# Encoder and cross attention in one program block, with batch 0's preparation queued inside the encoder's last step

## What is computed

```python
# 1. encoder of 6 layers: causal linear attention and an MLP, layer norm behind both
for l in range(N_LAYERS):
    q, k, v = x @ Wq[l] + bq[l], x @ Wk[l] + bk[l], x @ Wv[l] + bv[l]
    a = causal_linear_attn(elu(q) + 1, elu(k) + 1, v) @ Wo[l] + bo[l]
    x = layer_norm(x + a, g1[l], be1[l])
    x = layer_norm(x + gelu(x @ W1[l] + b1[l]) @ W2[l] + b2[l], g2[l], be2[l])
x = layer_norm(x, gf, bf)
x = _layernorm(x_in + x)
# 2. cross attention over ctx, 16 heads of 16, two softmax maps
attn = softmax(q1 k1 / scale) - gain * softmax(q2 k2 / scale)
o = attn @ vp                      # per head, then normalised per head
x = _layernorm(x + o @ wo.T)
# 3. feed-forward of three cycles
x = _layernorm(x + ffn(x))
```

## Time and profile before

| | us |
|---|---|
| median of 3 runs | 1772.83 (1771.63 to 1775.62) |
| the profiled execution | 1772.78 |
| its span | 1771.1 |
| TensorE busy | 1646.4 (93%) |
| VectorE busy | 1355.7 (77%) |
| ScalarE busy | 898.4 (51%) |
| GpSimd busy | 787.7 (44%) |
| DMA, mean over the span | 42 GB/s |

### The profile page before, as it was taken

How to read it: one execution, slowest core, us unless ns; L and a number is a source line. 1 busy time by engine, 2 the same in 40 slices (tenths; PEclk the granted TensorE clock), 3 DMA queues, 4 the chain that set the end, 5 groups by cost and what they waited for, 6 DMA issues and landing times. The chain is left out here.

```text
span 1771.1 us, 37461 instructions
## 1 busy us (share of the span) xinstructions
PE 1646.4 (93%) x15622; PEld 1330.7 (75%) x15622; DVE 1355.7 (77%) x2631; ACT 898.4 (51%) x1429; POOL 787.7 (44%) x580
## 2 busy tenths in 40 slices
PE   4899999999999999999999999999839999999598
PEld 4688888888888888888888888888725666665334
DVE  5778889888888888888888888888526777777346
ACT  2455554455554545545554455544216666665245
POOL 2343445434554435434553445533342555542325
PEclk8899999999999999999999999999959999999799
DMA  5100000100010000100001100100057777762001
GB/s 117 49 1 5 28 10 25 31 31 10 26 31 1 31 10 25 31 25 8 11 27 29 31 10 25 21 2 2 0 116 140 138 129 132 135 123 46 14 1 48
DMA packets 71704, 74.17 MB, mean 42 GB/s; under 512 B 18288, under 2 KB 57712, under 8 KB 71536
## 3 DMA queue, kind: packets, MB, share of 16 engines
q1 hardware_dynamic: 71536, 71.78, 19.6%
HBM read 57.08 MB, written 14.68 MB: 41 GB/s over the span
## 5 line engine op out<-in xcount | busy, mean ns | idle before, releaser
L629 POOL TENSOR_TENSOR e_h_lo<-e_h_f,e_h_hi 128x512 fp32r<-128x512 f32 x192 | 253.1, 1322 | 310.0 <-ACT e_h_hi L490 307.5
L714 DVE TENSOR_TENSOR e_am<-e_sc,c_amask 128x1024 f32<-128x1024 f32 x192 | 225.9, 1218 | 16.9 <-PE e_sc L365 16.6
L489 ACT ACTIVATE e_h_f<-e_pr,e_h_bias 128x512 f32<-128x512 f32 x192 | 132.2, 689 | 183.7 <-PE e_pr L166 179.6
L1394 DVE TENSOR_REDUCE x_mx<-x_psS 128x4 f32<-128x1024 f32 x128 | 155.0, 1221 | 66.3 <-PE x_psS L1112 65.9
L164 PE MATMUL e_pr<-e_yT_hi,e_W_hi 128*128 128x512 f32 x384 | 167.6, 437 | 0.3 <-DVE e_yT_lo L707 0.3
L164 PE MATMUL e_tr<-e_W_hi,e_h_hi 128*128 128x256 f32 x576 | 164.4, 285 | 1.4 <-issue 1.4
L166 PE MATMUL e_tr<-e_W_hi,e_h_lo 128*128 128x256 f32 x576 | 162.9, 283 | 0.0
L165 PE MATMUL e_tr<-e_W_lo,e_h_hi 128*128 128x256 f32 x576 | 161.6, 281 | 0.0
L1255 ACT ACTIVATE x_ex<-x_psT 128x1024 f32<-128x1024 f32 x128 | 131.1, 1024 | 57.8 <-PE x_psT L1138 56.9
L166 PE MATMUL e_pr<-e_yT_hi,e_W_lo 128*128 128x512 f32 x384 | 152.2, 396 | 0.0
L165 PE MATMUL e_pr<-e_yT_lo,e_W_hi 128*128 128x512 f32 x384 | 151.9, 396 | 0.0
(11 more groups left out here) (267 smaller groups left out, 4653.5 us busy)
## 6 DMA issues: line engine op xcount, KB each, us to landing
x_qs<-query_rows SPq DMA_DIRECT2D x128, 128.0 KB, 4.8
e_raw_m<-in_L_attn_W_dram SPq DMA_DIRECT2D x12, 1024.0 KB, 6.8
x_ks<-key_rows SPq DMA_DIRECT2D x64, 128.0 KB, 4.9
query_rows<-x_q_hi SPq DMA_DIRECT2D x16, 256.0 KB, 2.4
query_rows<-x_q_lo SPq DMA_DIRECT2D x16, 256.0 KB, 2.5
x_ctok<-in_ctx_dram SPq DMA_DIRECT2D x8, 256.0 KB, 5.4
x_xo<-in_x_dram SPq DMA_DIRECT2D x8, 256.0 KB, 2.8
key_rows<-x_k_hi SPq DMA_DIRECT2D x8, 256.0 KB, 4.9
```

Of the source, the lines that this page charges most:

```text
L489: act.activation(h_f[:, m % HR, :], ps_pr[m % 2][:, :], ACT.Gelu, bias=h_bias[:, m:m + 1])
L629: pool.tensor_tensor(h_lo[:, m, :], h_f[:, m % HR, :], h_hi[:, m, :].bitcast(F32), ALU.subtract).then_inc(h_lo_done, 1)
L714: dve.tensor_tensor(am[:, s % 2, c, :, :, :], ps_sc[:, :, c * 2 * P:(c + 1) * 2 * P].rearrange("p r (h n) -> p r h n", n=P), amask[:, :].u ...
L1394: dve.tensor_reduce(mx[:, N % 2, :, :].rearrange("p i (a h x) -> p h a i x", h=2, a=2)[:, pair, :, :, 0], ps_s[pair][:, :, :].rearrange("p ...
```

## The change

`cross` becomes `cross_stage`. It no longer opens a block; it returns functions for each engine, and the encoder's lists call them. So encoder and cross attention are one block without a meeting of the engines between them. The cross attention's tiles are now allocated from the right side of SBUF over the tiles that only the encoder's attention used (`att`), which nobody needs after step 22; SyncE waits for the last use of the two raw weight buffers before it loads `raw_wo`. The order of the PSUM tensors is changed so that `x_psS` lies on the four banks of `e_sc`: `early(0)` to `early(3)`.

- *Step 22:* VectorE makes the statistics of batch 0 ahead of the subtraction for `Wo`, and the block matrices (now one instruction) behind it.
- *Step 23, PE:* weights and context behind `mlp_down(1)`, values behind `mlp_down(3)`, transposes of x1 behind `mlp_up(1)`, the first query half behind `mlp_up(2)`, the second behind the step. The wait for the last gelu ahead of the last `mlp_down` is gone; `h_lo` is still waited for.
- *Step 23, the others:* as in the two places below. ScalarE copies weights, context and values ahead of the first gelu. The copies of x1 and of the queries for batch 0 go from ScalarE to VectorE. The zeroing of `vx` and `mx` goes from GpSimd to VectorE. The last `mlp_down`'s layer norm 2 is centred in slot 1 and scaled in slot 2. Batch 1's `encoder_norm` is split in `encoder_scale` and `encoder_add` and stands behind GpSimd's last `h_lo`.
- *Weights grouped:* the four weight products go to one bank and are copied at once, so are the two of the values and the four of `wo` (3 copies for 10).

```diff
+    att.close()
+    banks.close()
+    own.close()
+    nxt = cross_stage(nc, ctx, consts, X, inputs)
+    final = NT * L - 1
 
...
-            load_next(sp)
+            inputs.load(sp)
+            sp.wait_ge(o_lo, L)
+            sp.wait_ge(w2_lo, L)
+            nxt.sync(sp)
...
+                if u == final:
+                    pe.wait_ge(z_done[1], SB * NT * L)
+                    cross.weights()
+                    cross.context(0, cross.early(3))
...
+                if u == final:
+                    cross.values(0, cross.early(0))
...
                 if mlp:
                     mlp_up(0)
                     mlp_up(1)
+                if u == final:
+                    cross.x1_transpose(0, cross.early(1))
...
                     if mlp:
                         mlp_up(2 + s)
+                    if u == final and s == 0:
+                        cross.queries(0, 0, cross.early(2))
...
-            pe.wait_ge(yT_lo_done, 2 * NT * L)
-            pe.wait_ge(gelu_done, FC * NT * L)
+            cross.queries(0, 1, cross.early(3))
             for s in range(SB):
-                mlp_down(s, NT * L - 1, L)
+                mlp_down(s, final, L)
+            cross.items()
...
+                if u == final:
+                    cross.weights()
+                    cross.context(0, cross.early(3))
+                    cross.select()
...
+                    if u == final:
+                        cross.values(0, cross.early(0))
                     gelu(0)
...
+                if u == final:
+                    cross.encoder_scale(0)
                 if mlp:
                     rsqrt(1, ve_done[1], u + 1)
+                if u == final:
+                    pool.wait_ge(ln_done[1], SB * NT * L)
+                    cross.encoder_add(0)
+                    cross.x1_norm(0)
+                    cross.keys_lo(0)
...
+            cross.encoder_scale(1)
+            cross.encoder_add(1)
             rsqrt(2, ve_done[2], NT * L)
+            cross.items()
...
+                if u == final:
+                    residual(2, 0, d, last, m_full, xb2_done)
                 if mlp:
                     scale(1, u, q, rows_a["be1"])
+                if u == final:
+                    cross.sets()
...
-                if prev:
+                if prev and u < final:
                     residual(2, 0, d, last, m_full, xb2_done)
...
                 if prev:
                     residual(2, 1, d, last, m_full, xb2_done)
+                if u == final:
+                    cross.x1_stats(0)
+                    cross.value_weights()
+                if prev:
                     residual(2, 2, d, last, m_full, xb2_done)
...
+                if u == final:
+                    cross.x1_transposed(0, cross.early(1))
+                    cross.queries_hi(0, 0, cross.early(2))
+                    cross.queries_lo(0, 0, cross.early(2))
+                    scale(2, d, last, rows_m["be2"])
...
+                if u == final - 1:
+                    cross.encoder_stats(0)
...
+                if u == final - 1:
+                    cross.blocks()
...
+            cross.queries_hi(0, 1, cross.early(3))
+            cross.queries_lo(0, 1, cross.early(3))
+            cross.encoder_stats(1)
             for s in range(SB):
                 residual(2, s, final, NT - 1, m_full, xb2_done)
                 spread(2, s, final, NT - 1)
             moments(2, final)
-            centre(2, final, NT - 1, rows_m["g2"], ln2_rows_loaded, 32 * L)
-            scale(2, final, NT - 1, rows_m["be2"])
-
-    own.close()
+
+            def last_centre():
+                centre(2, final, NT - 1, rows_m["g2"], ln2_rows_loaded, 32 * L)
+
+            def last_scale():
+                scale(2, final, NT - 1, rows_m["be2"])
+
+            cross.items({1: last_centre, 2: last_scale})
+
+    nxt.own.close()
...
+    def early(i):
+        return ps_s[i // 2][:, i % 2, :]
...
+        def weights():
+            flat = bd[:, :, :, :].rearrange("p i h d -> p i (h d)")
+            pe.wait_ge(bd_done, 1)
             for k in range(MAPS):
                 for c in range(KC):
-                    pe.wait_ge(bd_done, (2 + k) * KC + c + 1)
-                    pe.matmul(bank(k * KC + c)[:, 0:P], bd[:, k * KC + c, :, :].rearrange("p h d -> p (h d)"),
-                              bd[:, (2 + k) * KC + c, :, :].rearrange("p h d -> p (h d)"), start=True, stop=True).then_inc(prep_full, 1)
+                    mm = pe.matmul(early(0)[:, blk(k * KC + c)], flat[:, k * KC + c, :], flat[:, (2 + k) * KC + c, :],
+                                   start=True, stop=True, skip_group_check=True)
+            mm.then_inc(prep_full, 1)
             for c in range(KC):
-                pe.wait_ge(bd_done, 4 * KC + c + 1)
-                pe.transpose(bank(4 + c)[:, 0:P], bd[:, 4 * KC + c, :, :].rearrange("p h d -> p (h d)"), ident[:, :]).then_inc(prep_full, 1)
+                mm = pe.transpose(early(1)[:, blk(c)], flat[:, 4 * KC + c, :], ident[:, :])
+            mm.then_inc(prep_full, 1)
             pe.wait_ge(wo_loaded, 16)
-            for n in range(KC):
-                for m in range(KC):
-                    i = n * KC + m
-                    if i >= 2:
-                        pe.wait_ge(prep_copied, i - 1)
-                    pe.transpose(bank(6 + i if i < 2 else i - 2)[:, 0:P], raw_wo[:, n, blk(m)], ident[:, :]).then_inc(prep_full, 1)
-            pe.wait_ge(prep_copied, 10)
-
-            def transpose_to(out, src):
-
+            for m in range(KC):
+                for n in range(KC):
+                    mm = pe.transpose(early(2)[:, blk(m * KC + n)], raw_wo[:, n, blk(m)], ident[:, :])
+            mm.then_inc(prep_full, 1)
...
+        def items():
             scores(0, 0)
+            pe.wait_ge(q_lo_done, KC)
             scores(0, 1)
...
+        def weights():
+            act.wait_ge(prep_full, 1)
+            act.activation(wqk[:, :, :, :].rearrange("p k c n -> p (k c n)"), early(0), ACT.Copy, scale=DH ** -0.5).then_inc(prep_copied, 1)
+            act.wait_ge(prep_full, 2)
+            act.activation(wv[:, :, :].rearrange("p c n -> p (c n)"), early(1)[:, 0:KC * P], ACT.Copy).then_inc(prep_copied, 1)
+            act.wait_ge(prep_full, 3)
+            act.activation(woT[:, :, :].rearrange("p c n -> p (c n)"), early(2), ACT.Copy).then_inc(prep_copied, 1)
...
+        def encoder_scale(e):
+            rsqrt(0, e)
+            pool.wait_ge(rows_loaded, 32)
+            if e > 0:
+                pool.wait_ge(x1_step, XS * (e - 1) + XS)
+            for s in range(QB):
+                pool.tensor_scalar(xw[:, s, :], X[:, e * QB + s, :], mv[0][:, s, 0:1], rs[0][:, s:s + 1],
+                                   ALU.subtract, ALU.mult).then_inc(x1_step, 1)
+            pool.wait_ge(x1_step, XS * e + QB)
+            pool.tensor_tensor(xw[:, :, :], xw[:, :, :], gf[:, :].unsqueeze(1).broadcast_to([P, QB, D]), ALU.mult).then_inc(x1_step, 1)
+
+        def encoder_add(e):
+            pool.wait_ge(xo_loaded, 16 * e + 16)
+            pool.tensor_tensor(xo[:, :, :], xo[:, :, :], bf[:, :].unsqueeze(1).broadcast_to([P, QB, D]), ALU.add).then_inc(x1_step, 1)
+            pool.wait_ge(x1_step, XS * e + QB + 2)
+            pool.tensor_tensor(xw[:, :, :], xw[:, :, :], xo[:, :, :], ALU.add).then_inc(xadd_done, 1)
...
+        def x1_transposed(e, bank):
+            dve.wait_ge(x1_tr, e + 1)
+            dve.tensor_copy(x1T[:, :, :].rearrange("p c n -> p (c n)"), bank).then_inc(x1T_done, 1)
+
+        def queries_hi(e, c, bank):
+            dve.wait_ge(q_full, KC * e + c + 1)
+            dve.tensor_copy(q_hi[:, c, :], bank).then_inc(q_hi_done, 1)
...
+        def blocks():
+            dve.wait_ge(w_loaded, 16 * 6)
+            dve.tensor_tensor(bd[:, :, :, :], raw_w[:, :, :, :].rearrange("p i c d -> p (i c) d").unsqueeze(2).broadcast_to([P, 5 * KC, HC, DH]),
+                              headmask[:, :].unsqueeze(1).unsqueeze(3).broadcast_to([P, 5 * KC, HC, DH]), ALU.mult).then_inc(bd_done, 1)
+            dve.tensor_scalar(neg_gain[:, :], gain[:, :], -1.0, None, ALU.mult)
...
+        def sets():
             dve.memset(first_rows[:, :, :], 0.0).then_inc(sets_done, 1)
-            encoder_stats(0)
+            dve.memset(vx[:, :, :, :, HX:HP], 0.0)
+            dve.memset(vx[:, :, :, :, DH:HX], 1.0)
+            dve.memset(mx[:, :, :, :], 0.0).then_inc(zeros_set, 1)
             dve.wait_ge(sets_done, 1)
             for pair in range(2):
                 for a in range(2):
                     r = a * HALF + pair * HP
                     m = dve.memset(first_rows[r:r + 1, pair, :], 1.0)
...
+        def value_weights():
+            w = wv[:, :, :].rearrange("p c (h d) -> p (c h) d", d=DH)
+            dve.wait_ge(prep_copied, 2)
+            dve.tensor_reduce(wv_sum[:, :], w, AX.X, ALU.add).then_inc(sets_done, 1)
+            dve.wait_ge(sets_done, 3)
```

(7 more changed lines are left out.)

728 lines of the change are left out of this document (338 added, 390 removed).

## The result

The changed kernel takes **1725.26 us** (median of 4 runs, 1723.98 to 1727.0), the kernel before 1773.92 in the same series (4 runs, 1771.63 to 1775.62): ratio 0.9727, 95% interval 0.971 to 0.9744. The profiled execution took 1723.98 us, its span 1722.3.

What follows compares the result with a forecast made beforehand. The bound was a 46.0 us engine-to-engine chain between the last encoder matmul and the first score matmul. Gain 46.0 - 6.9 (end of encoder) - 0.2 (after first score) = 38.9 us, from 1772.83 to 1733.9 us; range 1729 to 1742.

Steps and rivals of the forecast that it cites:

- the end of the encoder: Encoder's last two steps: taking in batch 0's preparation makes PE free for scores 6.9 us later.
- PE's moved work, 6.4: Encoder's last two steps: batch 0's products, transposes and query halves cost PE 5.8 us, 6.4 with changes of matmul kind.
- Step 22, +0.7, and `bd`: VectorE in step 22: batch 0's statistics delay PE 0.7 us; block matrices take about 1.5, 1.1 of it in idle time.
- The new wait, 1.6 instead of 0.6: Last step, before the MLP input's transposes: PE waits 1.6 us for VectorE's third residual instead of 0.6, +1.0.
- Given back, -1.4: Before the last `mlp_down`: the second query half fills PE's 1.40 us wait for the last gelu, -1.4.
- Queries in time, cover 0.8 to 2.8: At the first score: keys and query rows are back from DRAM 0.8 to 2.8 us before PE asks; nothing paid.
- After the first score, +0.2: First slots: residual and moments +0.9, centring and scaling 0 to 1, full PE clock -0.7; net +0.2 us.
- queries late: Rival, at the first scores: query chain slips by 8 us, idle PE falls to 1.2 GHz; 1740 us, chance 0.12.
- The stretched step: Rival, last encoder step: GpSimd blocks nine two-input VectorE operations, 1.04 us each, +9.4 us; 1743 us, chance 0.10.
- The slower clock through the whole cross attention: Rival: without its long rest PE stays at 1.2 GHz, 0.7 us per slot over 64 slots; 1777 us, chance 0.02.

Runs made afterwards that it cites:

- place_only: Kernel before with only the encoder's tiles put at the changed kernel's SBUF addresses: 1764.26 us, ratio 0.9943.
- zeros_later: Changed kernel with VectorE's zeroing of the cross attention's rows moved from ahead of the third residual to behind the first query half: 1722.40 us, ratio 0.971.

## Why the prediction was wrong

It failed on a sentence that had no number: "On both sides of it the kernel runs at its own pace, which the change does not touch." The encoder's 23 steps became 8.33 us faster in the profile, 9.4 us in the runs, by where its tiles stand. The diff showed the new allocation; the working read it only as memory for the cross attention. No rival had the encoder in it, so the range had no room: the forecast without it was 1733.9, and 1733.9 - 8.3 = 1725.6 against 1725.26 measured.

The rest came out at the forecast, by luck in part. From the row of step 22 to the end of the span the changed kernel takes 521.9 us and place_only, which has the same pace, 560.9: 39.0 us against 38.9. But the end of the encoder cost 5.8 us instead of 6.9, and behind the first score 1.6 us were lost (447.3 against place_only's 445.7) instead of 0.2; the two errors cancel. Term by term (times of the kernel after are compared with those before less the 8.33):

1. *PE's moved work, 6.4.* Too much: by start times it measured 1239.84 - 1237.94 = 1.90 for weights and context, 0.81 for the values, 0.36 for x1 and 0.67 and 0.68 for the two query halves, **4.4** in all. The query halves were priced at 2.0 and took 1.35, the transposes at 1.8 and took 1.37, the products at 2.0 and took 1.70. The changes of kind were there: the encoder's next matmul follows late behind each group (1255.66 - 1255.24 = 0.42 us behind the first query half, where 0.23 is usual), some 0.4 in all where 0.6 were expected.
2. *Step 22, +0.7, and `bd`.* Right for PE: it waited 1.75 us for the last query rotation, 0.76 more than the 0.99 of place_only. Too little for VectorE: the one instruction for `bd` took 2.48 us. The 1.5 did not follow from its rows, for the ten old ones took 2.31 together. So the first residual of the attention is 1.9 us late (1231.70 against 1238.09 - 8.33), where 0.7 and 0.4 were expected.
3. *The new wait, 1.6 instead of 0.6.* Right in kind, 2.43 us in size. The third residual is 4.2 us late, 4.8 were expected; PE was there sooner because its own work was shorter. The zeroing held the residual, as the step had it, but GpSimd's sum of the batch's input was ready only 0.4 us before VectorE was, as zeros_later shows.
4. *Given back, -1.4.* Right: no wait before the last `mlp_down`. The end of the encoder is 1275.15 - (1278.45 - 8.33) = 5.0 us late, not 6.9. This flatters the change a little, since the faster pace goes on behind the row of step 22; against place_only it is (1275.15 - 1200.39) - (1268.14 - 1199.16) = 5.8.
5. *Queries in time, cover 0.8 to 2.8.* In time, but only just. The eight loads were issued from 1264.30 on, the last one landed at 1274.44 by the trace, 0.6 us ahead of PE. SyncE's delay was there (7.2 us from store to loads), and PE came sooner than the working had it.
6. *After the first score, +0.2.* It was 1319.21 - 1275.04 = 44.2 us to the first scores of slot 9, against 1367.69 - 1324.45 = 43.2: **+0.9**. The moments did delay the first maxima by about 1 us. The full clock that should have given 0.7 was not there: after only 2.06 us of rest it fell to 0.50 for 10 us, and slot 1 took 1282.94 - 1277.85 = 5.09 us, exactly as before. It was back at 1.00 at 1288, behind 10 us of work with waits of under 0.5 us. The Trainium skill (TensorE: Matmul & The Clock Gate, "What's actually happening") says that activity releases the throttle; the trace agrees.

The rivals: queries late, not seen, though 0.6 us of cover is thin. The stretched step did not occur in the changed kernel (VectorE's four centring operations took 1.66 us), and occurred one small edit away; VectorE's scaling, four operations in 4.41 us, was slowed too but off the path. The slower clock through the whole cross attention did not occur.
